# A block-product scheme on seven instead of six of eleven tiles, with row copies moved to GpSimd

## The reference, cut to what matters

```
x  = x + attention(layernorm(x), ctx)
xn = layernorm(x)
xq = clip(round(xn / sx), -128, 127) * sx               # sx from max |xn| over all rows
gate, up = xq @ Wg_quant.T, xq @ Wu_quant.T              # 1408 outputs each, from 512
h  = silu(gate) * up ;  hq = the same rounding, sh from max |h|
out = x + hq @ Wd_quant.T
```

## Time and profile before

| what | value |
|---|---|
| median of 3 runs | 1239.04 us (1238.58 to 1240.55) |
| the profiled execution's own time | 1239.66 us |
| its span in the trace | 1237.9 us |
| PE busy | 1230.6 us, 99% of the span, granted clock 1.0 |
| VectorE, ScalarE, GpSimd busy | 1052.5, 858.5 and 381.1 us |
| the stretch of pairs | about 826 to 1041 us of the span |

### The profile page before, as it was taken

One profiled execution on the slowest core, in us unless ns is written; L12 is line 12 of the kernel. 1 busy time (PEld: TensorE's weight loads), 2 busy tenths in 40 slices (PEclk: granted clock), 3 DMA queues, 4 the chain that ended last, 5 costly groups with the idle time before them and its releaser, 6 DMA issues.

```text
span 1237.9 us, 20617 instructions
## 1 busy us (share of the span) xinstructions
PE 1230.6 (99%) x7500; PEld 573.2 (46%) x7500; DVE 1052.5 (85%) x1917; ACT 858.5 (69%) x1349; POOL 381.1 (31%) x295
## 2 busy tenths in 40 slices
PE   8999999999999999999999999999999999999998
PEld 5544444444444444444444444544444444444444
DVE  7976988988988898898898868889999998888777
ACT  6888577657757757756765763468888885399760
POOL 0113343144044134224314420224444443022223
PEclk9999999999999999999999999999999999999999
DMA  8284346256254363462462483398976854199996
GB/s 315 86 255 171 95 137 209 66 159 190 79 178 152 111 191 108 120 222 69 137 228 79 119 236 131 139 289 242 278 239 228 272 183 154 47 372 414 423 426 261
DMA packets 174565, 241.74 MB, mean 195 GB/s; under 512 B 122608, under 2 KB 142080, under 8 KB 156928
## 3 DMA queue, kind: packets, MB, share of 16 engines
q1 hardware_dynamic: 174432, 240.42, 58.5%
q10 hardware_dynamic: 32, 0.01, 0.0%
HBM read 120.86 MB, written 90.57 MB: 171 GB/s over the span
## 4 chain that ended last, share of the span: by engine, by line
PE 93%; ACT 3%; DVE 2%; DMA 1%; issue 1%; SPq 1%; ACTq 0%
PE bank L2502 12%; PE po L81 10%; PE po L83 9%; PE po L82 9%; PE bank L2379 8%; PE ring L83 8%; PE ring L82 8%; PE ring L81 8%; PE bank L2384 4%; PE bank L2385 4%; PE bank L2360 3%; PE bank L2341 3%; PE ring L1257 2%; PE ring L1284 2%; DMA x<-in_x_dram 1%; ACT E L479 1%
## 5 line engine op out<-in xcount | busy, mean ns | idle before, releaser
L81 PE MATMUL ring<-yT,M 128*128 128x512 f16 x512 | 194.1, 379 | 0.0
L82 PE MATMUL ring<-yT,M 128*128 128x512 f16 x512 | 194.0, 379 | 0.0
L83 PE MATMUL ring<-yT,M 128*128 128x512 f16 x512 | 194.0, 379 | 0.0
L81 PE MATMUL po<-VW,p 128*128 128x512 f16 x480 | 182.2, 380 | 0.0
L82 PE MATMUL po<-VW,p 128*128 128x512 f16 x480 | 181.9, 379 | 0.0
L83 PE MATMUL po<-VW,p 128*128 128x512 f16 x480 | 181.9, 379 | 0.0
L494 ACT ACTIVATE p<-E 128x512 f16<-128x512 f32 x120 | 74.8, 625 | 122.7 <-DVE E L741 122.7
L414 POOL TENSOR_TENSOR esum<-E 128x512 f32<-128x512 f32 x16 | 23.4, 1462 | 409.2 <-DVE p L745 369.6
L417 POOL TENSOR_TENSOR esum<-esum,E 128x512 f32<-128x512 f32 x96 | 129.5, 1349 | 51.2 <-ACT E L483 18.4
L2502 PE MATMUL bank<-w,hb 128*128 128x512 f16 x605 | 131.3, 379 | 0.0
L1989 ACT ACTIVATE hb<-hb,hscale 128x512 int8<-128x512 f32 (+1 forms) x155 | 95.2, 709 | 16.7 <-DMA hb<-hidden 13.4
(11 more groups left out here) (389 smaller groups left out, 2492.9 us busy)
## 6 DMA issues: line engine op xcount, KB each, us to landing
xa<-x_rows_d SPq DMA_DIRECT2D x28, 1024.0 KB, 6.9
hidden<-hb SPq DMA_DIRECT2D x22, 1024.0 KB, 9.1
hb<-hidden SPq DMA_DIRECT2D x18, 1024.0 KB, 9.8
x<-in_x_dram SPq DMA_DIRECT2D x16, 1024.0 KB, 5.2
value_fold<-E SPq DMA_DIRECT2D x64, 256.0 KB, 2.5
VW<-value_fold SPq DMA_DIRECT2D x16, 1024.0 KB, 6.5
x_rows_d<-x SPq DMA_DIRECT2D x16, 1024.0 KB, 6.0
out_dram<-xa SPq DMA_DIRECT2D x11, 1024.0 KB, 11.6
```

What stands on the lines that cost most here:

```text
L81: nc.tensor.matmul(out, a_hi, b_hi, start=first, stop=False)
L82: nc.tensor.matmul(out, a_hi, b_lo, start=False, stop=False)
L83: return nc.tensor.matmul(out, a_lo, b_hi, start=False, stop=last)
```

## The change

The joint tiles are now those with i % 3 != 1, which are 0, 2, 3, 5, 6, 8 and 9, and the single ones 1, 4, 7 and 10. So three times in a pair (2 and 3, 5 and 6, 8 and 9) two joint tiles are adjacent, and the last tile of a pair is a single one. The cut diff (`taken_joint`, `made_joint` and the waits follow the new order by tables; the sums of weights are made in eight pieces instead of four, since the joint tiles lie at 0, 3, 6, 9 and 2, 5, 8):

```
-    JOINT = tuple(range(0, FT, 2))
+    JOINT = tuple(i for i in range(FT) if i % 3 != 1)
+    SINGLE = tuple(i for i in range(FT) if i % 3 == 1)
+    ahead = lambda i: i > 0 and i - 1 in JOINT
...
+    BY_POOL = 5
+    xq_of = lambda g: xq_apart if g == 2 else xq_odd if g >= BY_POOL and g % 2 else xq[:]
...
+    def rows_of_pair(p):
+        early = {5: (2 * p + 3, 3)}
+        late = {2: (2 * p + 3, 1), 3: (2 * p + 3, 2), 6: (2 * p + 4, 0), 8: (2 * p + 4, 1), 9: (2 * p + 4, 2)}
+        if p == 1:
+            early[2] = (2 * p + 3, 0)
+        else:
+            early[0], late[0] = (2 * p + 2, 3), (2 * p + 3, 0)
...
+        def round_row(g, t):
+            pool.wait_ge(x_normed, TT * (g - 1) + t + 1)
+            if g > BY_POOL:
+                pool.wait_ge(x_turned[g % 2], 64 * ((g - 1) // 2))
+            nc.gpsimd.tensor_copy(xq_of(g)[:, t], ints_of(g)[:, t]).then_inc(rows_rounded, 1)
         for p in PAIRS:
             for i in JOINT:
                 add_fourth(p, i)
+                if i in early:
+                    round_row(*early[i])
+                if i in late:
+                    round_row(*late[i])
                 joint_hidden_b(p, i)
```

ScalarE's loop:

```
         for p in PAIRS:
             for i in JOINT:
-                seed(p, i)
+                if not ahead(i):
+                    seed(p, i)
                 keep_third(p, i)
...
                 joint_silu_a(p, i)
-                if i < JOINT[-1]:
+                if i + 1 in SINGLE:
                     single_silu(p, i + 1, 0)
-                if i in late and late[i][0] < NG:
+                if i in late:
                     normalise_row(*late[i])
+                if i + 1 in JOINT:
+                    seed(p, i + 1)
                 keep_fourth(p, i)
```

PE's loop:

```
             for i in JOINT:
-                if joint(p, i) == 0 or i > 0:
+                if not ahead(i):
                     joint_first(p, i)
                 joint_third(p, i)
...
                 joint_middle(p, i)
-                if i < JOINT[-1]:
+                if begins:
                     single_product(p, i + 1, 0)
                     single_product(p, i + 1, 1)
                 else:
-                    single_product(p, i - 1, 3)
-                    if p + 1 in PAIRS:
-                        pe.wait_ge(x_turned[0], 64 * (p + 1))
-                        joint_first(p + 1, 0)
+                    single_product(*half_made, 3)
+                    joint_first(p, i + 1)
                 joint_late(p, i)
```

More of the change, by code:

```diff
@@ L1509, in ffn @@
     PAIRS = range(1, NG // 2 - 1)
-    JOINT = tuple(range(0, FT, 2))
+    JOINT = tuple(i for i in range(FT) if i % 3 != 1)
+    SINGLE = tuple(i for i in range(FT) if i % 3 == 1)
     NJ, NS = len(JOINT), FT - len(JOINT)
     ALL_J, ALL_S = NJ * len(PAIRS), NS * len(PAIRS)
-    joint = lambda p, i: NJ * (p - 1) + i // 2
-    TAKEN = ("seed", "third", "silu_a", "fourth", "silu_b")
+    joint = lambda p, i: NJ * (p - 1) + JOINT.index(i)
+    ahead = lambda i: i > 0 and i - 1 in JOINT
     def order_of_products():
@@ L1519, in order_of_products @@
         for K in range(ALL_J):
-            if K == 0 or K % NJ:
+            if not ahead(JOINT[K % NJ]):
                 made.append(("first", K))
@@ L1525, in order_of_products @@
             made += [("second", K), ("gate_a", K)]
-            if K % NJ == NJ - 1 and K + 1 < ALL_J:
+            if ahead(JOINT[(K + 1) % NJ]):
                 made.append(("first", K + 1))
@@ L1533, in ffn, with order_of_takes @@
     made_joint = lambda what, K: MADE[what, K]
[L1535 to L1542, removed]
+    def order_of_takes():
+        taken = []
+        for K in range(ALL_J):
+            if not ahead(JOINT[K % NJ]):
+                taken.append(("seed", K))
+            taken.append(("third", K))
+            if K > 0:
+                taken.append(("silu_b", K - 1))
+            taken.append(("silu_a", K))
+            if ahead(JOINT[(K + 1) % NJ]):
+                taken.append(("seed", K + 1))
+            taken.append(("fourth", K))
+        taken.append(("silu_b", ALL_J - 1))
+        return {take: n + 1 for n, take in enumerate(taken)}
+    TAKEN = order_of_takes()
+    taken_joint = lambda what, K: TAKEN[what, K]
+    single = lambda p, i: NS * (p - 1) + SINGLE.index(i)
     wide_w = w[:, 0:2].rearrange("p j n -> p (j n)")
@@ L1598, in ffn @@
     w_summed, x_normed, x_summed = sem("weights_summed"), sem("x_normed"), sem("x_summed")
+    rows_rounded = sem("rows_rounded")
+    row_rounded = lambda g, t: TT * (g - BY_POOL) + t + 1
+    def rows_of_pair(p):
[5 more added lines that the diff above has]
+            early[0], late[0] = (2 * p + 2, 3), (2 * p + 3, 0)
+        return [{i: row for i, row in rows.items() if row[0] < NG} for rows in (early, late)]
     joints, joints_taken = sem("joint_products"), sem("joints_taken_by_scalar")
@@ L1700, in turn @@
             elif g // 2 > 2:
-                sp.wait_ge(joints, made_joint("gate_b", joint(g // 2 - 2, JOINT[-1])))
+                sp.wait_ge(singles, 4 * NS * (g // 2 - 2))
             for t in range(TT):
@@ L1710, in store_h @@
                 p = g // 2
-                sp.wait_ge(single_hs, 2 * (single(p, m1 // 2 * 2 - 1) + 1))
-                sp.wait_ge((j_hs_a, j_hs_b)[g % 2], joint(p, (m1 - 1) // 2 * 2) + 1)
+                sp.wait_ge(single_hs, 2 * (single(p, max(i for i in SINGLE if i < m1)) + 1))
+                sp.wait_ge((j_hs_a, j_hs_b)[g % 2], joint(p, max(i for i in JOINT if i < m1)) + 1)
             sp.dma_start(h_d[g][:, m0:m1], hb[:, HOME[g], m0:m1]).then_inc(h_stored[HOME[g]][c], 16)
@@ L1767, in on_sync @@
         load_r(ODD)
-        sp.wait_ge(joints, made_joint("gate_b", ALL_J - 1))
+        sp.wait_ge(singles, 4 * ALL_S)
         load_r(1)
@@ L2462, in on_tensor @@
         for p in PAIRS:
+            pe.wait_ge(x_turned[0], 64 * p)
             pe.wait_ge(x_turned[1], 64 * (p + 1))
             for i in JOINT:
-                if joint(p, i) == 0:
-                    pe.wait_ge(x_turned[0], 64 * p)
-                if joint(p, i) == 0 or i > 0:
+                if i > 0:
+                    half_made = (p, i - 1) if i - 1 in SINGLE else None
+                else:
+                    half_made = (p - 1, SINGLE[-1]) if p - 1 in PAIRS else None
+                begins = i + 1 in SINGLE
+                if not ahead(i):
                     joint_first(p, i)
@@ L2471, in on_tensor @@
                     up(1, FT - 1, ("up",))
+                if half_made:
+                    single_product(*half_made, 2)
                 if i > 0:
[L2473 to L2476, removed]
-                    single_product(p, i - 1, 3)
+                    joint_close(p, JOINT[JOINT.index(i) - 1])
+                elif p - 1 in PAIRS:
+                    joint_close(p - 1, JOINT[-1])
+                if half_made and begins:
+                    single_product(*half_made, 3)
                 joint_middle(p, i)
-                if i < JOINT[-1]:
+                if begins:
                     single_product(p, i + 1, 0)
```

138 lines of the change are left out of this document (73 added, 65 removed).

## The result

The change is slower: 1241.97 us (median of 13 runs, 1241.48 to 1243.65) against 1239.34 us for the kernel before (13 runs), a ratio of 1.0023 with a 95% interval of 1.0014 to 1.0031. The forecast was 1241.8.

A forecast was written before the change was run, and what follows sets the result against it. PE's dense matmul stream was taken to bound the kernel. Terms -2.59 - 0.68 + 2.5 + 3.55 gave +2.8 us, forecast 1241.8 us from the 1239.66 us profiled run (median 1239.04); 8-in-10 range 1236.5 to 1244.8.

The forecast's parts named there:

- What bounds the kernel: PE, busy 99% of the span, issues matmuls without gaps but for 0.14 us a pair; other engines have room.
- The twelve slots and the old gap: One tile a pair goes from 16 to 14 matmuls, -2.59 us; the stall between pairs goes, 5 x 0.135, -0.68 us.
- slot: PE's time for one matmul, 0.2158 us; 164 a pair make 35.39 us, 162 make 34.96.
- The prediction's second paragraph: Between pairs, the product after up_a's last matmul waits for the seed: slots end at 863.11, it starts at 863.25.
- The places where joint tiles meet: At gate_b, released late by the copy of fourth: 17 stalls of 0.11 us plus 0.64 in pair 1, +2.5 us.
- The sums beside GpSimd: Before tile 9's fourth product: GpSimd's addition and copy (0.8 us) delay VectorE's sums; stall c - 0.09, pairs 1-5, +3.55 us.
- The sum: All terms over the whole kernel: -2.59 - 0.68 + 2.5 + 3.55 = +2.8 us, forecast 1241.8 us.
- no change: Chance given to a measured time within 0.2% (2.5 us) of the kernel before: 0.39.
- What costs nothing: VectorE loses eleven casts without gain; added ScalarE and GpSimd work fills idle time; odd group's transposes land at 31.9, before the first sum.
- the second sum didn't go ahead of the copy: Rival at VectorE's sums: it keeps the port, second sum precedes GpSimd's copy, stall 0.08, 1238.7 us; chance 0.27.
- Neither stalls: Rival where joint tiles meet: the seed comes in time or copy order hides it too, 1236.7 us; chance 0.16.
- no transposes came late: Rival in pairs 1 and 2: slow transposes delay first sum and cross, twice 1.2 us, 1244.2 us; chance 0.12.

The follow-up runs named there:

- second_first: Against the change: PE makes the second product of the second tile ahead of gate_b where two joint tiles meet; 1239.67 us, 1.0004 to the kernel before.
- fourth_first: Against the change: ScalarE copies fourth ahead of the next tile's seed where two joint tiles meet; 1241.02 us, 1.0014 to the kernel before.
- copy_moved: Against the change: GpSimd's copy of tile 8 is done at tile 9, ahead of that tile's own; 1245.69 us, 1.0051 to the kernel before.
- cast_vector: Against the change: seven joint tiles kept, but VectorE casts whole groups and GpSimd copies nothing; 1249.37 us, 1.0078 to the kernel before.
- copy_twice: Against the change: each GpSimd copy of tile 8 is issued twice, first to an unused row; 1242.63 us, 1.0025 to the kernel before.
- reach_later: Against the change: second product before gate_b, second sum behind tile 9's cross, pair 1's row moved, tile 6's reach behind the fourth sum; 1237.24 us, 0.9982 to before.
- sum_behind_cross: Against the change: VectorE's second sum stands behind the cross of tile 9 instead of ahead; 1240.17 us, 1.0006 to the kernel before.

## Why the prediction was right, point by point

**What bounds the kernel**: right. PE's stream is dense but for its waits, and each edit here moved the time by what it did to the distance of pairs.

**The twelve slots and the old gap**: right. With nearly all gaps gone the distance came down to 35.10, from 35.53. Two readings behind these terms need a remark. Eight matmuls in 1.73 us give 0.216 and not yet the 0.2158 of a slot; the 44 slots in 9.50 us of second_first bear it out. And the wait for the copy of fourth in the earlier trace rows cost PE nothing: the old gap stands behind it, in front of the product at 863.25, whose weight load the profile puts down to no other engine:

```profile
PEld bank L2384 <- issue: 2.2, 5, 0.4
```

The prediction's second paragraph, which has that product wait for the seed, fits this, and so does fourth_first, where the order of before brings the gap of before back.

**The places where joint tiles meet**: forecast 0.11 us each, measured 0.116; forecast 0.64 for pair 1's tile 2, measured 0.64. The cause is shown by second_first: two slots more in front of gate_b, and the gaps are gone but for 0.21 us in pair 1.

**The sums beside GpSimd**: the mechanism was right (first sum behind the addition, copy behind the first sum, second sum behind the copy). I forecast about 1.4 us for each sum at a copy of 0.8; they took 1.47 and 1.09. The copy was mis-sized: 0.61 us instead of 0.8, and of its two bounds the memset's 0.53 was the nearer one, not the select's 0.88. By the prediction's own formula that is 0.61 - 0.09 = 0.52 a pair; measured 0.58. The rest is the release at the end: the prediction gave PE 0.06 us after the cross, as after ScalarE's copy of fourth, but the cross ends at 894.88 and the matmul starts at 895.03, 0.15 later. Its own rows had that figure: the seed ended at 863.10 and the product behind it started at 863.25. The term was 2.9 us, not 3.55.

The Trainium skill, page "GPSIMD Engine Reference", section "Performance versus the Vector engine", gives 769 ns for a tight loop over 512 elements; the prediction's estimate of 3.4 us from it was too high as well, since this copy took 613 ns.

What the prediction didn't see is that the copy was not the culprit but the queue: had it not stood there, the hidden block would have, for twice as long (copy_moved).

**The sum**: 2.2 us by the rows where 2.8 were forecast, and 2.6 between the medians. That the total came within 0.2 us of the median was luck: with the true copy the forecast would have been 1240.9. Two things hid this in part: the longer release behind the cross adds 5 x 0.06 = 0.3, and the median of three runs of the kernel before, on which the forecast stands, lay 0.3 under that of thirteen. Its size lay at the bound of 0.2%, and I gave 0.39 to no change; that was fair.

**What costs nothing**: right for VectorE's load, which fell without effect, and for the transposes, which landed ahead of the first sum (no wait of a sum on a DMA in the trace after). cast_vector shows how thin this is: there a sum waits for a transpose three times, 1.6 us in all.

**The rivals**: the second sum didn't go ahead of the copy; the engines take turns, as copy_twice shows best. "Neither stalls" needed edits of its own, and no transposes came late.

## What to carry to other kernels

Matmuls taken from a full stream are worth their slots only if the chain of copies between their products still fits the slots that remain: count it at each place where the order of products gets tighter, and look for an independent product to put in between. When two operations of VectorE in a row read SBUF on both inputs, ask what GpSimd has queued at that moment: here whatever it was, a copy or a hidden block, ran between them; put such a pair apart, or behind what PE waits for. After a cure read the distance between repeats again, because the next link of the same chain may be only a little less late.

## What the runs showed of the hardware that was not expected

- GpSimd and VectorE take turns under this exclusion: with two copies and two sums queued they ran sum, copy, sum, copy (1.48, 1.08, 1.09 and 1.07 us, each its own time plus the other's rest), so a longer GpSimd queue did not hold VectorE for longer than one operation. It is the order of issue: the second sum is issued at 894.01, when the first ends (894.09), and the second copy at 894.50, when the first one ends (894.56), so neither engine had two in a row.
- GpSimd's copy of 128x512 from int8 to f16 takes 0.61 us, half of its addition of two f32 operands of that size (1.27 us), and four of them move the work of a VectorE cast of 1.22 us.
- VectorE's operations on a PSUM and an SBUF operand kept 0.69 us while GpSimd ran (L2144 at 894.19 beside the hidden block, and 0.68 to 0.70 in all 42 cases), as did its reach (1.20 to 1.21 us in all 66). Those with both inputs in SBUF waited, and so did casts: before, the cast at 867.61 beside the addition at 867.14 took 1.89 us where others took 1.22.
- Where the operation waited for wrote a PSUM bank, PE started later behind it than where it wrote SBUF. From VectorE's cross, in after (894.88 to 895.03) and reach_later (865.99 to 866.14), and from ScalarE's seed, before (863.10 to 863.25), it is 0.15 us to the matmul. From ScalarE's copy of fourth (862.62 to 862.67, before) and VectorE's third sum (898.00 to 898.05, sum_behind_cross) it is 0.05 to the weight load. Which of the two differences makes the 0.1 us, the memory written or what waits, no run here tells.
